# Attention of layer 0 and 1: score operands without zero rows, two heads in 64-row tiles, half of the key/value products moved

## The reference, cut to what matters

```
x = x + tanh(g) * attention0(layernorm(x), ctx)   # 16 heads of 8, causal mask (strictly lower, key 0 for query 0)
x = x + tanh(g) * experts0(layernorm(x))          # 6 experts of 100 tokens each, top 1
x = x + tanh(g) * attention1(layernorm(x), ctx)   # 8 heads of 64, no mask
x = x + tanh(g) * moe1(x')                        # 8 experts of 512, top 2 per batch, layer norm
attention0: scores = q k^T / sqrt(8); softmax over 256 keys; probs v; W_o
```

## Time and profile before

| | us |
|---|---|
| median of 3 runs | 287.31 |
| lowest, highest run | 284.59, 287.57 |
| span of the profiled execution, first to last instruction | 285.0 |
| mean granted PE clock, share of full | 0.941 |

### The profile page before, as it was taken

The page is one execution under the profiler, slowest core; times in us unless marked ns, Lnnn a source line. Parts: engine busy times, 40 slices in busy tenths (PEclk is TensorE's granted clock), DMA queues, the critical chain, the costliest instruction groups (busy, mean ns, idle before and its releaser), DMA issues.

```text
span 285.0 us, 4711 instructions
## 1 busy us (share of the span) xinstructions
PE 234.1 (82%) x1686; PEld 178.3 (63%) x1686; DVE 200.8 (70%) x498; ACT 136.7 (48%) x345; POOL 94.2 (33%) x129
## 2 busy tenths in 40 slices
PE   0912889489889999879789699989979968999992
PEld 0712655366666575668668477867757746799891
DVE  4699975458886435998847988796997983245643
ACT  2610434146455664435539657676655621726440
POOL 4699300033434353033445623231241150021111
PEclk9965999979999999999999989999999975999998
DMA  7830999600000000000000000000400401300510
GB/s 193 226 31 22 204 217 222 115 0 5 3 3 2 5 0 2 0 1 2 0 0 0 3 0 2 1 0 0 149 0 3 147 1 18 133 0 2 166 30 25
DMA packets 11986, 13.79 MB, mean 48 GB/s; under 512 B 1028, under 2 KB 9988, under 8 KB 11676
## 3 DMA queue, kind: packets, MB, share of 16 engines
q1 hardware_dynamic: 11676, 12.96, 18.7%
q10 hardware_dynamic: 288, 0.54, 0.9%
HBM read 9.70 MB, written 2.88 MB: 44 GB/s over the span
## 4 chain that ended last, share of the span: by engine, by line
PE 56%; DVE 28%; DMA 7%; ACT 3%; issue 2%; SPq 2%; POOL 1%; POOLq 0%; DVEq 0%; ACTq 0%
PE PS L1194 7%; PE PS L1241 6%; PE PS L1255 5%; DVE XH L714 5%; PE PS L1226 4%; PE PS L1134 4%; DVE QK L820 4%; PE PS L1210 3%; DMA QK<-MT 2%; DVE MX L808 2%; DMA X<-in_x 2%; PE PS L1056 2%; PE PS L1060 2%; PE PS L1109 2%; DVE MX L751 2%
## 5 line engine op out<-in xcount | busy, mean ns | idle before, releaser
L751 DVE TENSOR_REDUCE MX<-PS 128x2 f32<-128x512 f32 (+1 forms) x48 | 31.7, 686 | 13.1 <-PE PS L1091 7.7
L1194 PE MATMUL PS<-KT,VA 128*128 128x256 f32 x128 | 32.3, 396 | 1.4 <-ACT VA L652 1.3
L456 POOL TENSOR_TENSOR QK<-QK,RC 128x512 f32<-128x512 f32 x16 | 16.7, 1042 | 44.7 <-DVE RC L816 44.7
L595 ACT ACTIVATE QK<-PS,NM 128x256 f32<-128x256 f32 x64 | 29.4, 477 | 1.1 <-DVE NM L810 1.1
L1194 PEld LDWEIGHTS PS<-KT,VA 128*128 128x128 f32 x128 | 23.7, 195 | 8.6 <-issue 4.1
L446 POOL TENSOR_SCALAR_AFFINE_SELECT PT<-PT 128x512 f32<-128x512 f32 x16 | 10.1, 634 | 54.3 <-ACT PT L575 54.3
L571 ACT ACTIVATE PT<-PS 128x1024 f32<-128x1024 f32 x16 | 16.4, 1023 | 24.1 <-PE PS L1109 24.1
L808 DVE TENSOR_REDUCE MX<-PS 128x4 f32<-128x1024 f32 x16 | 19.5, 1218 | 11.7 <-PE PS L1194 11.6
L409 POOL TENSOR_SCALAR VE<-MV 128x2 f32<-128x2 f32 x20 | 5.2, 259 | 64.7 <-DVE MV L704 64.7
L820 DVE TENSOR_SCALAR QK<-QK,RC 128x256 f32<-128x256 f32 x32 | 25.4, 832 | 0.6
L714 DVE TENSOR_SCALAR XH<-X,MV,RS 128x128 f32<-128x128 f32 x32 | 20.2, 1018 | 2.3 <-POOL RS L410 2.3
(11 more groups left out here) (175 smaller groups left out, 544.4 us busy)
## 6 DMA issues: line engine op xcount, KB each, us to landing
QK<-in_w SPq DMA_DIRECT2D x8, 512.0 KB, 4.2
QK<-qk_scr SPq DMA_DIRECT2D x3, 768.0 KB, 9.0
qk_scr<-V SPq DMA_DIRECT2D x2, 768.0 KB, 7.7
W<-in_w SPq DMA_DIRECT2D x1, 768.0 KB, 7.4
QK<-PARTS SPq DMA_DIRECT2D x12, 64.0 KB
qk_scr<-PARTS SPq DMA_DIRECT2D x1, 768.0 KB, 5.4
X<-in_x SPq DMA_DIRECT2D x2, 256.0 KB, 5.5
CT<-in_ctxT SPq DMA_DIRECT2D x2, 256.0 KB, 6.8
```

The source lines that it names most:

```text
L456: g_.tensor_tensor(pr, pr, RC1[:, n % 2, 2:4].unsqueeze(2).to_broadcast([P, 2, S]), ALU.mult).then_inc(s_p1p, 1)
L595: last = a.activation(PR[:, n % 3, h, it, :], banks(2 * (n % 2) + h)[:, it * S:(it + 1) * S], ACT.Exp, scale=D1 ** -0.5, bias=NM1[:, n % 2 ...
L751: v.tensor_reduce(dst, banks(n % 2).rearrange("p (h j) -> p h j", j=w), AXX, ALU.max, negate=True).then_inc(s_mx0, 1)
L1194: last = mm(banks(2 * (n % 2) + h)[:, it * S:(it + 1) * S], QT1[:, c, h, it * P:(it + 1) * P], KT1[:, c, b * S:(b + 1) * S], start=True, s ...
```

## The change

- `QK` has 8 heads x 256 tokens side by side in partitions 0 to 49 and the other 8 in partitions 64 to 113; no zero rows are written or used (`KS` = 50 rows in the transposed scores, `KR` = 48 in the others). Products of two heads, one at row 0 and one at row 64, follow each other and write different PSUM banks.
- A unit of `scores0` is two banks (0 and 1), 6 units per batch, one or two per step by turns, and waits for the maxima of the unit just before it. `maxima0` reduces 1024 columns.
- `scores0T` comes in two halves of two heads (384 columns in bank 2, 384 in bank 3), the first where it was, the second behind `outputs0`; each waits until ACT has read the half before it. `exps0` is two operations of 768 columns.
- `outputs0` uses banks 4 and 5 by turns; `heads_out` moves from DVE to ACT.
- Batch 0's parts go through the scratch as those of the others: `split_out(0)`, `split_in(0)` ahead of the rest. Each `split_in` is two transfers (48 partitions each, runs of 4 KB), each transfer of maxima too. The staging areas lie in a pool of their own.
- Eight `kv` are in the prologue, between the projections (`PROLOGUE`), eight in steps -6 to -1, none later; W1 is loaded ahead of the second half of the context; expert_tokens(2) moves into the prologue.
- x is loaded in three transfers, the gates apart from the other vectors; POOL writes the constants of VA at the very start.

```diff
-KV_LATE = 4 * B - 9
-KV_BANK = [6] * 3 + [4, 5, 6] * 2 + [m % 2 for m in range(KV_LATE)]
-KZ = 96
+KS = KR + 2
+KV_FIRST = 8
+KV_BANK = [m % 2 for m in range(KV_FIRST)] + [6, 4, 5, 6, 4, 5, 6, 4]
+UNITS = ((1, 0), (1, 1), (0, 0), (1, 2), (1, 3), (0, 1))
...
+def units(g):
+    t = g - M0
+    if t >= 4 * B:
+        return []
+    n = NU * (t // 4) + (0, 1, 3, 4)[t % 4]
+    return [n, n + 1] if t % 2 else [n]
+
+PROLOGUE = (("project", 0), ("project", 1), ("kv", 0), ("tokens", 0), ("kv", 1), ("project", 2), ("kv", 2),
+            ("tokens", 1), ("kv", 3), ("project", 3), ("kv", 4), ("tokens", 2), ("kv", 5), ("kv", 6), ("kv", 7))
...
             def split_in(b):
-                sp.wait_ge(s_zero, b + 1)
                 sp.wait_ge(d_scr[b], 16)
+                for r in range(2):
+                    src = qk_scr[b].rearrange("a k (d q h) t -> q (k d) a (h t)", q=2, d=D0)
+                    sp.dma_start(QK[64 * r:64 * r + KR, :, b, :], src[r]).then_inc(d_qk[b], 16)
+            split_out(0)
+            split_in(0)
             split_out(1)
             split_out(2)
             split_in(1)
             split_out(3)
             split_in(2)
+            sp.dma_start(WO0[:, :], wo0).then_inc(d_late, 16)
             split_in(3)
...
-            g_.memset(QKZ[:, 0, 0:H0 * S // 2], 0.0).then_inc(s_zero, 1)
+            g_.memset(VA[:, :, :, 8:9], 1.0)
+            g_.memset(VA[:, :, :, 9:32], 0.0).then_inc(s_va0, 1)
             for b in range(B):
                 rstd(b)
-            for b in range(1, B):
-                zero_qk(b)
...
             def exps0(n):
                 if n >= 3:
                     act.wait_ge(s_av0, n - 2)
+                for i, (full, done) in enumerate(((s_sta, s_pa), (s_stb, s_p0))):
+                    act.wait_ge(full, n + 1)
+                    a.activation(PT0[:, n % 3, i:4:2, :],
+                                 banks(2, 1024).rearrange("p (r n) -> p r n", r=2)[:, :, 0:384],
+                                 ACT.Exp, scale=D0 ** -0.5).then_inc(done, 1)
...
             def scores0(n):
+                b, u = divmod(n, NU)
+                it, k = UNITS[u]
+                hw = 4 - 2 * it
+                if n == 0:
+                    pe.wait_ge(s_k1c, KV_FIRST)
                 if u == 0:
+                    pe.wait_ge(d_qk[b], 32)
+                if n >= 1:
+                    pe.wait_ge(s_mx0, n)
+                for r in range(2):
+                    ... mask product into bank r, as before ...
+                w = S if it else P
+                for g in range(hw):
+                    for r in range(2):
+                        rows = slice(64 * r, 64 * r + KR)
+                        last = mm(banks(r)[:, g * w:(g + 1) * w], QKh[rows, 0, b, hw * k + g, it * P:(it + 1) * P],
+                                  QKh[rows, 1, b, hw * k + g, 0:w], start=False, stop=True, skip_group_check=True)
                 last.then_inc(s_s0, 1)
...
+            def scores0T(n, i):
+                b, hg = divmod(n, 4)
+                if i == 1:
+                    pe.wait_ge(s_pa, n + 1)
+                elif n:
+                    pe.wait_ge(s_p0, n)
+                h = 2 * hg + i
+                for r in range(2):
+                    rows = slice(64 * r, 64 * r + KS)
+                    mm(banks(2 + r)[:, 0:S], QKh[rows, 1, b, h, 0:P], QKh[rows, 0, b, h, :],
+                       start=True, stop=True)
+                for r in range(2):
+                    rows = slice(64 * r, 64 * r + KS)
+                    last = mm(banks(2 + r)[:, S:S + P], QKh[rows, 1, b, h, P:2 * P], QKh[rows, 0, b, h, P:2 * P],
+                              start=True, stop=True)
+                last.then_inc(s_stb if i else s_sta, 1)
...
             for g in STEPS:
+                for i in units(g)[:1]:
+                    scores0(i)
                 if 0 <= g < 4 * B:
+                    scores0T(g, 0)
...
                 for m in kvs(g):
                     kv(m)
                 if 2 <= g < 4 * B + 2:
                     outputs0(g - 2)
+                for i in units(g)[1:]:
+                    scores0(i)
+                if 0 <= g < 4 * B:
+                    scores0T(g, 1)
                 if g >= 4 and g % 2 == 0 and (g - 4) // 2 < 2 * B:
                     transpose_heads((g - 4) // 2)
```

More of the change, by code:

```diff
@@ L716, in apply_norm @@
                 last.then_inc(s_xh, 1)
-            v.memset(QKZ[:, 1, 0:H0 * S // 2], 0.0).then_inc(s_zero_k, 1)
-            for half in ((0, 1), (2, 3)):
-                dve.wait_ge(d_x[half[0] // 2], 16)
-                for b in half:
+            for batches in ((0, 1), (2, 3)):
+                for b in batches:
+                    dve.wait_ge(d_x[min(b, 2)], 16)
                     stats(x_tiles(b))
-                for b in half:
+                for b in batches:
                     apply_norm(0, b)
@@ L928, in _ @@
                 n = g - A1
-                if g < M0 + 4 * B:
-                    for i in range(3):
-                        maxima0(3 * (g - M0) + i)
-                if g >= 3 and g % 2 == 1 and (g - 3) // 2 < 2 * B:
-                    heads_out((g - 3) // 2)
+                for i in units(g):
+                    maxima0(i)
                 if g >= 4 and g % 2 == 0 and (g - 4) // 2 < 2 * B:
@@ L1033, in _ @@
             pe.wait_ge(d_c, 16)
-            for b in range(B):
-                project(b)
-                if b == 1:
-                    expert_tokens(0)
-            expert_tokens(1)
             def kv(m):
@@ L1111, in scores0T @@
-                last.then_inc(s_sta, 1)
-                if n >= 1:
-                    pe.wait_ge(s_p0, n)
-                for g in range(4):
-                    h = 4 * hg + g
-                    last = mm(banks(4)[:, g * P:(g + 1) * P], QKh[0:KZ, 1, b, h, P:2 * P],
-                              QKh[0:KZ, 0, b, h, P:2 * P], start=True, stop=True)
-                last.then_inc(s_stb, 1)
+                if i == 0 and hg == 0:
+                    pe.wait_ge(d_shift[b], 32)
+                    if b == 0:
+                        pe.wait_ge(d_one, 32)
+                        pe.wait_ge(s_vpc, ELT)
@@ L1133, in outputs0 @@
                         src = PT0[:, n % 3, g, 0:256] if jt == 0 else PT0[:, n % 3, g, 256:384]
-                        last = mm(banks(5)[rows, half + jt * P:half + S], VA[:, 2 * b + jt, 4 * hg + g, :], src,
+                        last = mm(banks(4 + n // 2 % 2)[rows, half + jt * P:half + S], VA[:, 2 * b + jt, 4 * hg + g, :], src,
                                   start=(jt == 0), stop=(jt == 1), skip_group_check=True)
@@ L1379 @@
     c[:, C_IOTA:C_IOTA + NE] = np.arange(NE, dtype=fp)
-    by_feature = lambda w: w.reshape(D, H0, D0).transpose(0, 2, 1).reshape(D, D)
+    heads = np.array([[4 * (h // 2) + 2 * r + h % 2 for h in range(H0 // 2)] for r in range(2)])
+    by_feature = lambda w: w.reshape(D, H0, D0)[:, heads, :].transpose(0, 3, 1, 2).reshape(D, D)
     arrays = {
```

207 lines of the change are left out of this document (70 added, 137 removed).

## The result

The changed kernel takes **292.4 us** (median of 5 runs, 291.4 to 294.4), the kernel before 287.6 (5 runs, 284.6 to 289.5). The ratio is 1.019, 95% interval [1.012, 1.026]: slower by nearly 2% (1.7% by the medians). The kernel before has a quicker and a slower kind of execution, and every ratio here compares the quicker ones. The profiled execution has a span of 291.7 us against 285.0, +6.7; it is the longest of the five (spans 289.7 to 291.7, the middle one 290.4), so about 1 us of the 6.7 is its own.

A forecast was written before the change was run, and what follows sets the result against it. It took the kernel as stages with separate limits: zero fills in the prologue, DMA from 34 to 57 us, then PE. -3.2 + 2.9 + 0.4 + 1.8 = +1.9 on 285.0 gives 286.9, plus 2.3 to the median 289.2; range 282.0 to 296.0.

The forecast's parts named there:

- Prologue and transfers: Up to the first transposed scores: zero fills gone, batch 0 through the scratch, scores at 53.7 instead of 56.9 us, -3.2.
- the returns: Transfers back from the scratch in the prologue: four, one behind the other in one queue, 4.8 us each.
- The bound that I wrote for PE: Prologue, if returns are fast: first unit at about 30, ten units 21 us, scores at 51 us, -5.9.
- Steps 0 to 9: From the first transposed scores to step 10: 35.5 us against 32.6, +2.9.
- The turns: Score units and DVE reductions alternate instead of overlapping: 1.93 us with 256-key heads, 2.36 with 128-key heads.
- the clock, set at 0: Granted clock: a shorter wait before the first transposed scores could spare 1.2 us at most; taken as 0.
- Steps 10 to 16: From step 10 to the experts0 stage: 22.5 us against 22.1, +0.4.
- The ping-pong with ACT: Steps 10 to 16: halves of the transposed scores take turns with ACT's exponentials, 2.8 us per step, 16.7 for six.
- Changes of shape: Some 38 more tile-shape changes on PE at 0.09 us, about half hidden: +1.8, bounds 0 and +6.
- rival B: Row tiles on PE run one behind the other (294 us) or drain at each change (293), both 298; chance 0.16.
- Rival A: Returns overlap, tile changes are free, PE stays warm: 283.5 us; or steps keep their old pace: 281; chance 0.24.
- Rival C: The clock falls during the steps, with 48 of 128 rows working and PE waiting more: +10 or more, 300; chance 0.08.

The follow-up runs named there:

- late_kv: The changed kernel with one key/value product in the prologue instead of eight and seven of them in steps 10 to 16: 297.1 us, ratio 1.029.
- x_early: The changed kernel with X tiles 2 and 3 (batch 1) loaded second, ahead of W0 and the context: 292.2 us.
- units_pp: The changed kernel with the nine score units before step 0 alternating between two pairs of banks: 289.6 us (286.3 to 292.3, of four).
- odt_early: The changed kernel with ACT doing each step's events before the second exponential and the copy of head outputs last: 284.5 us.
- t_free: The changed kernel with the second half of the transposed scores in banks 0 and 1 from step 10 on: 292.1 us.
- rows48: The kernel before with its layer-1 score products reading 48 rows (transposed scores 50) instead of 96, zero fills kept: 297.9 us, ratio 1.037.
- no_zeros: The kernel before without zero rows or fills, score products over 48 and 50 rows, constants of VA written first: 291.1 us, median of twelve in two groups.
- one_bank: The changed kernel with score units of one bank and one row half, double-buffered as before: four executions, 288.8, 293.3, 304.1 and 304.9 us.

## Why the prediction came out as it did

The forecast was 289.2 in 282 to 296, the result 292.4: within the range, slower by 1.7% where I had given within 1% and slower nearly the same chance. The forecast's sum was +1.9 in the span; it was +6.7. The 4.8 between them are some 6.6 for the clock (an estimate, worked out below), which the sum had at 0, less the 1.8 that it had for changes of shape. That the time still lies in the range owes something to its width.

**Prologue and transfers, -3.2: the number right, the holder wrong.** The first transposed scores came at 53.69 where I had said 53.7. But the ring was idle from about 50.5, 27.4 us behind the first return's issue at 23.15 where the sum has 30.2, so the returns were shorter than the 4.8 us that it took, and ten units from 32.9 on, most of them turns of 2.0 to 2.3 us, held the scores. The bound that I wrote for PE, 30 plus 21, was the actual case: its 21 was right (20.8), its start at 30 was too early by 2.9, as the eight products do not cost nothing there (late_kv starts 3.1 earlier), and the x of batch 1 came late (x_early, -2.3). units_pp shows that the turns held. Two errors cancelled, which was luck. That the two partition halves serialise, which I had weighed from the Trainium skill, is left open by these runs.

**Steps 0 to 9, +2.9: measured +5.3.** The turns were right: 2.03 us where I had 1.93, 2.26 where I had 2.36. So was the step with ODT. Taken in pairs from the first transposed scores (odd step and the even one behind it; I had 6.3, up to 6.9, and 1.7 + 0.5 more in steps 7 and 8):

| steps | 1, 2 | 3, 4 | 5, 6 | 7, 8 | 0 and 9 |
|---|---|---|---|---|---|
| expected | 6.3 | 6.3 to 6.9 | 6.9 | 9.1 | 6.3 |
| measured | 8.3 | 6.9 | 7.3 | 9.1 | 6.4 |

2.0 of the 2.4 missing lie in steps 1 and 2, where the clock is at 1.2 GHz from 56.5 to 64.5. The term that failed is the clock, set at 0: by the price above its 10.2 us at half are 2.6, and without them the stretch would take about 35.4 (an estimate), the 35.5 of the sum.

**Steps 10 to 16, +0.4: measured +2.7.** ODT cost 1.8 each (1.7 expected). The missing 2.3 us go with the half clock from 98.5 to 105, behind a pause in which PE waits for ODT, and again at 114.5: 7.7 us at half, 1.9 by the price. odt_early took away the waits of 3.7 and with them another 1.6, which bears this out without separating it fully. The ping-pong with ACT was not the limit that I took it for (t_free: 24.8, perhaps 1 us less at like clock). That the seven products bring nothing here was right for the reason given, that PE waits anyway; late_kv adds that putting them back costs 8.7 in this stretch.

**Changes of shape, +1.8: the size right, the place on the path wrong.** Steps 3 to 8 come out within 0.4 us without them, so here they lie where PE waits anyway. In units_pp the two mask products start at 32.25 and the four row-tile products at 32.56, 0.31 us later, of which 0.22 are streaming: a gap of 0.09. The next full-array product starts 0.32 after that, which is 0.09 and two times 0.11: the four products of 0.11 ran as two pairs side by side. The Trainium skill (TensorEngine Tiling (Array Packing), "Key Properties") says a change of mode drains the engine; here a drain would show as the gap of 0.09 us, at most, and rival B falls. Where PE is the limit the gaps do count: in rows48 they are 0.1 each and bring 1.1 us in steps 10 to 16. Rival A was half true: the returns took less than I had said, but the turns stood behind them, and PE did not stay warm.

**After the logits** the span has 1.9 us more, for which the sum had nothing. It is the clock again: 21.7 us at half where the kernel before has 16.4, 5.3 more, about 2.1 by the price above (an estimate). Whether this part of the loss belongs to the change is not settled, since kernels that do not differ there have from 10.4 to 21.7 us at half.

**Rival C**, the clock, was the mechanism that was missing, at 0.08 and with +10; in the changed kernel it is 4.5 us in steps 0 to 16 and 2 more behind the logits, by the price above (an estimate). I had argued against it that with PE busy the clock holds. That was read from a kernel whose products had 96 rows. rows48 shows that the argument does not carry over: 10 us more, with PE busy 41.07 of 42.22 us. The Trainium skill (TensorE: Matmul & The Clock Gate, Part 1) ties the clock to how busy the engine has been; these traces show PE busy for 3.00 of 3 us and the clock at half, for 20 us and more. What the chip counts, no run here shows. How much of the changed kernel's half clock comes from its 48 rows, two tiles of them side by side, how much from the short stops at changes of shape and how much from its pauses, was not separated. So it is shown what the clock costs here, but not why it falls.

## What to carry over

Ask of every late small copy which queue it stands in and behind what: moving ACT's events ahead of the second exponential and of the copy of head outputs brought 7.9 us, more than the whole change was about. In these traces a pause of PE is often followed by work at half clock; count both. When kernels share a stretch of work, set its time against its time at half clock before explaining a difference by anything else. Rows of zeros that look like waste can go with a clock that comes back when PE is the limit; before they go, the version with only the rows changed is the cheap test.

## What was not expected of the hardware

- A PE that is busy without a break over 48 rows at 1.2 GHz stayed there for 20 us (rows48), 34 us (no_zeros, its slower group) and 48 us (one_bank); over 96 rows, in the kernel before, it was back at 2.4 GHz after 3.4 us. It also fell with PE busy, 1.00 and 0.86 of the two us ahead in rows48. The 48 rows bring a stop of 0.1 us at each change of shape with them, and which of the two it is stays open. In two of these kernels it happened in some executions only: no_zeros 286.8 to 288.8 or 293.4 to 296.2.
- Behind the logits, where six of these kernels do the same, the time of the stretch follows the time at half clock: 10.4 us at half and 170.8, 16.1 and 173.1, 21.7 and 175.3.
- Raising the mean clock made the kernel no faster by itself: 0.957 to 0.979 at 300.4 us, against 0.93 at 292.4.
- Row tiles of two times 48 rows run side by side at 0.11 us per pair of 256 columns, with 0.09 us on changing from the full array.
